# The down products of an MLP block stand two blocks behind its gate and up products instead of one

## The reference, cut to what matters

```
h    = rmsnorm(x_normed, ln1_w)
h    = x_normed + mamba2(h, ...)          # in-projection, conv, scan in chunks of 128, out-projection
h2   = rmsnorm(h, ln2_w)
mlp  = silu(h2 @ gate_w.T) * (h2 @ up_w.T) @ down_w.T      # 512 -> 1792 -> 512
x    = x + layernorm(h + mlp)
# second sublayer: x @ W_up.T plus, for the one of 4 experts that a token picks, a LoRA of rank 8
x    = x + layernorm(ffn(layernorm(x)))
```

## Time and profile before

| | |
|---|---|
| median of 3 executions | 876.89 us (876.71 to 879.94) |
| profiled execution, its own time | 876.88 us |
| its span, first to last instruction | 874.8 us |
| mean granted TensorE clock | 0.965 of full speed |
| PE busy | 793.5 us, 91% |
| DVE busy | 488.4 us, 56% |
| ACT busy | 340.1 us, 39% |
| POOL busy | 201.4 us, 23% |

### The profile page before, as it was taken

One profiled execution on the slowest core, in us unless ns is written; L12 is line 12 of the kernel. 1 busy time (PEld: TensorE's weight loads), 2 busy tenths in 40 slices (PEclk: granted clock), 3 DMA queues, 4 the chain that ended last, 5 costly groups with the idle time before them and its releaser, 6 DMA issues.

```text
span 874.8 us, 15284 instructions
## 1 busy us (share of the span) xinstructions
PE 793.5 (91%) x5712; PEld 557.5 (64%) x5726; DVE 488.4 (56%) x1138; ACT 340.1 (39%) x627; POOL 201.4 (23%) x236
## 2 busy tenths in 40 slices
PE   3857597898999999999999999999999999999945
PEld 3634375566865777567855786567756785677632
DVE  6476565548663576447544665357644765455343
ACT  2443356542552236323651345323632364222211
POOL 3445535531220123101230122002410123000000
PEclk9888789999999999999999999999999999999986
DMA  9920000000000200020001000020002000000010
GB/s 326 386 97 1 1 1 1 25 25 1 1 1 1 73 2 1 1 73 0 0 0 46 26 0 0 0 72 0 0 0 72 0 0 0 24 25 1 2 48 24
DMA packets 15541, 29.70 MB, mean 34 GB/s; under 512 B 1296, under 2 KB 1424, under 8 KB 15504
## 3 DMA queue, kind: packets, MB, share of 16 engines
q1 hardware_dynamic: 15504, 29.21, 9.5%
HBM read 25.01 MB, written 4.19 MB: 33 GB/s over the span
## 4 chain that ended last, share of the span: by engine, by line
PE 63%; issue 13%; DVE 10%; POOL 7%; ACT 4%; DMA 1%; SPq 0%; DVEq 0%; POOLq 0%; ACTq 0%
PE gu L1121 23%; PE wa L1121 19%; PE acc L1121 12%; PE wc L1121 5%; POOL y L445 2%; POOL weights L402 2%; PE wa L1144 2%; POOL ra L429 1%; DVE xbc L879 1%; DMA weights<-in_w_in 1%; DVE sg L965 1%; DVE stats_a L834 1%; DVE hn L856 1%; DVE hn L848 1%; DVE weights L982 1%
## 5 line engine op out<-in xcount | busy, mean ns | idle before, releaser
L1121 PE MATMUL gu<-h2t,weights 128*128 128x256 f16 x2688 | 312.9, 274 | 2.9 <-issue 2.9
L1121 PEld LDWEIGHTS gu<-h2t,weights 128*128 128x128 f16 x2688 | 260.9, 98 | 51.7 <-issue 17.9
L1121 PE MATMUL acc<-weights,act 128*128 128x512 f16 x672 | 165.2, 382 | 13.9 <-DVE act L970 13.9
L965 DVE SCALAR_TENSOR_TENSOR sg<-gu,bound,sg 128x256 f32<-128x256 f32 x112 | 53.5, 478 | 126.5 <-ACT sg L641 126.2
L1121 PE MATMUL wa<-ht,weights 128*128 128x256 f16 x960 | 113.9, 278 | 7.3 <-ACT conv_pad L576 4.3
L1121 PEld LDWEIGHTS wa<-ht,weights 128*128 128x128 f16 x960 | 95.7, 100 | 26.5 <-ACT conv_pad L576 4.5
L1121 PEld LDWEIGHTS acc<-weights,act 128*128 128x128 f16 x672 | 65.0, 98 | 72.2 <-DVE act L970 16.0
L641 ACT ACTIVATE sg<-gu,scale_inv 128x256 f32<-128x256 f32 x112 | 53.1, 474 | 146.5 <-PE gu L1121 146.3
L651 ACT ACTIVATE act<-sg 128x256 f16<-128x256 f32 x112 | 46.6, 416 | 139.8 <-DVE sg L965 138.9
L879 DVE SCALAR_TENSOR_TENSOR xbc<-conv_pad,conv_ws,xbc 128x256 f32<-128x256 f32 x144 | 65.8, 498 | 41.7 <-ACT conv_pad L576 31.5
L970 DVE TENSOR_TENSOR act<-sg,act 128x256 f16<-128x256 f32 x112 | 51.2, 457 | 54.9 <-ACT act L651 54.9
(11 more groups left out here) (182 smaller groups left out, 918.0 us busy)
## 6 DMA issues: line engine op xcount, KB each, us to landing
xa<-in_x SPq DMA_DIRECT2D x8, 512.0 KB, 3.5
weights<-in_x SPq DMA_DIRECT2D x8, 512.0 KB, 4.1
out_x<-h SPq DMA_DIRECT2D x16, 256.0 KB, 2.1
weights<-in_w_gate SPq DMA_DIRECT2D x3, 1024.0 KB, 13.1
weights<-in_w_up SPq DMA_DIRECT2D x3, 1024.0 KB, 14.5
weights<-in_w_down SPq DMA_DIRECT2D x3, 1024.0 KB, 13.9
weights<-in_w_in SPq DMA_DIRECT2D x5, 512.0 KB, 7.1
w_out_t<-in_w_out SPq DMA_DIRECT2D x1, 1024.0 KB, 15.3
```

What stands on the lines that cost most here:

```text
L965: nc.vector.scalar_tensor_tensor(sg[:, f % 2], GU[f % 2][:, SEQ:2 * SEQ], up_to_act, sg[:, f % 2], ALU.mult, ALU.mult).then_inc(sem("prod_ ...
L1121: return nc.tensor.matmul(dst, left, right, start=start, stop=stop)
```

## The change

On PE alone, the order within stage B changes. `b_down(f)` is issued after `b_gu(f + 2)` instead of after `b_gu(f + 1)`. Block 1 no longer has a `b_down` in it, and two of them stand behind block 13. No instruction is added or taken away, and the other engines' queues stay as they are.

```
                     if b is not None:
                         b_gu(b, f)
-                        if f:
-                            b_down(b, f - 1)
+                        if f >= 2:
+                            b_down(b, f - 2)
                     if a is not None and f in A_AT:
                         A_AT[f](a)
                     if c is not None and f in C_AT:
                         C_AT[f](c)
                 if b is not None:
+                    b_down(b, FBLK - 2)
                     b_down(b, FBLK - 1)
```

## The result

The changed kernel takes 884.20 us (median of 5, 883.08 to 885.03), the kernel before 877.76 us in the same comparison (median of 5). The ratio is 1.0072, with a 95% interval of 1.0054 to 1.0090: slower by 6.3 us, between 4.7 and 7.9. The forecast was 884.7 us and +7.8. The profiled execution took 884.76 us, its span is 883.0.

A forecast was written before the change was run, and what follows sets the result against it. PE's matmuls and few waits were taken as the bound, PE being busy 94.21 of 95.30 us in a full step. Terms 7.8 + 0.9 - 0.86 = +7.8 on 876.88 gave 884.7 us, eight-in-ten range 879.5 to 887.5.

The forecast's parts named there:

- The start of steps 2 to 7, +1.30 us each: Before `a_t1`: PE arrives 1.30 us earlier but `hn` does not, so the wait grows from 0.35 to 1.65 us.
- The middle of a step, nothing: Middle of a full step: between A's pieces PE still does one gate and up block and one down product; no change.
- The stalls of step 1: Step 1: PE's 13.2 us of waits for `act` stay as waits for A's inputs or other work; nothing gained.
- The clock term of step 1, +0.9 us: Step 1: PE restarts later, at 111.02, so gate and up 2 runs at low clock; +0.25 to +1.5, taken as +0.9 us.
- The end, -0.9 us: Last step with a B: down 13's wait for `act` goes, covered by downs 11 and 12; -0.86 us.
- The reading of the 2.24 us stall: Before 204.70: the clock stayed at 1.00 after 2.24 us, so the 1.65 us waits were given no clock loss.
- One small sum of the rivals: Step 1, its stalls partly on the path: some 4 or 5 of 13.2 us come back, about 879.5 us; chance 0.07.

The follow-up runs named there:

- The start alone: Kernel before, with no down product in block 1 and two in block 2, the rest in the old order: 886.91 us, ratio 1.0117.
- three blocks: Changed kernel with down products three blocks behind in every step: 886.96 us, ratio 1.0112 to the kernel before.
- the five kernels with moves on DVE: Kernels reordering DVE's queue (centring and scaling before block 0's product, statistics before `b_mlp`, or both), one or two blocks behind: ratios 0.9984, 1.0187, 1.0073, 0.9905, 1.0055.
- The end alone: Kernel before, with only down 12 moved behind `a_t2`, next to down 13: 876.98 us against 876.60, ratio 1.0000.
- Step 1 only: Down products two blocks behind in step 1 alone, one block behind elsewhere as in the kernel before: 877.12 us against 877.13, ratio 1.0001.
- Filling the wait: Changed kernel with 28 more unused matmuls on PE between gate and up 1 and `a_t1` of step 1: 881.54 us, ratio 1.0060 to the kernel before.
- the fastest kernel: Changed kernel with DVE's centring and scaling ahead of block 0's product and statistics ahead of `b_mlp`: 868.25 us, ratio 0.9905 to the kernel before.

## Why the prediction was right, and where it was off

**The start of steps 2 to 7, +1.30 us each: right, and shown.** The trace has 7.9 us in the six steps where the sum had 7.8, and the wait is 1.67 us (1.49 in step 2) where 1.65 was forecast. *The start alone* shows the place, *three blocks* the size of the next wait, the five kernels with moves on DVE the cause: `hn` stands in DVE's queue behind a product that hangs on PE's own gate and up 0, so PE cannot come to it sooner by leaving work out.

**The middle of a step, nothing: right.** *The end alone* leaves a full step at 95.30 us.

**The stalls of step 1: right in kind.** None of the 13.2 us came back; they joined the waits for `hn`, `ra` and the scan, as the growth of these in the waits after shows. The prediction said that an A piece waits there for DVE; the profile names POOL for `ra` and for the scan's `hn`. *Step 1 only* gives a ratio of 1.0001.

**The clock term of step 1, +0.9 us: mis-sized.** The step said "between 114.4 and 116.9" for the end of the low clock, and its bounds were +0.25 to +1.5. Measured in the trace were +1.8, of which 1.56 lie in gate and up 2 (its start to the next start: 4.74 us against 3.18). The clock was 0.50 from 111 to 116 and 0.91 from 116 to 120, so it was low until 116.7, which is 6.1 us after PE's restart at 110.63. Before, it was 5.9 us after the restart at 108.00. The prediction had this 5.9 from the same place and the 3.4 from another stall, and took the middle; the upper value was the right one. The rest was not foreseen: the 5.42 us wait before the scan and the one of 2.06 us drop the clock twice more, and gate and up 9 at 172.82 takes 3.73 us. PE, slowed there, reaches the out-projection at 184.20 with no wait for `y` before it, 13.05 us after the scan's product at 171.15; in *three blocks*, where the clock held, `y` ends the wait 12.74 us after it (168.51 to 181.25). So the second drop costs 0.3 us. *Filling the wait* takes 3.0 us out of the trace.

**The end, -0.9 us: right** (-0.86 in the trace). The experiment that was to show it alone was built on too simple a picture, as told above.

**The reading of the 2.24 us stall was too strong.** The prediction took from one row that a stall of this length leaves the clock alone. *The end alone* has the same stall with the clock falling. For the six full steps of the changed kernel this made no difference, they kept a clock of 1.00 behind 1.67 us; in step 1 the pause of 2.06 us lost it. Of 2.24 us the five profiles show both outcomes, of 2.06 us seven do, and no run here settles at what length the loss begins.

**The total.** The sum of +7.8 stands against +6.3 by the ratio (4.7 to 7.9) and +7.9 between the two profiled executions. The terms of the trace add up to 8.2. Part of the difference is the choice of execution: the profiled one has the longest span of the changed kernel's five, 1.2 us above their median of 881.8, while the 874.8 before is also the median of 21 spans of that kernel. By the medians of the spans the loss is 7.0 us. What is left is smaller than step 1's term, which the runs of *step 1 only* do not show in the time either; the clock behind the 2.24 us stall is a possible reason, not a settled one. That the forecast met the profiled difference to 0.1 us is in part luck: step 1's term was 0.9 us too small there, and the part ahead of it (-0.4), the part behind the last down product (-0.2) and the time outside the span (-0.3) took it back. One small sum of the rivals is off: with 4 or 5 us of step 1 gained back the time would be 879.7 to 880.7, not 879.5.

## What to carry to other kernels

Before work is taken out from between two points of the busiest engine, look at which wait has the least slack behind it, and what starts that wait's chain: if the chain starts at the same engine's work just ahead, leaving out filler buys nothing, and the filler has to be paid for elsewhere. A longer software delay gives slack to one consumer (`act`) and takes cover from another (`hn`); it pays only when the freed slack is then spent, here by letting the other queue put the uncovered producer first. And where stalls are merged rather than removed, count the low clock from the later restart: the matmuls that ran between the stalls no longer help to bring it back, and others pay for it.

## What the runs showed of the hardware

The same pause of PE of 2.24 or 2.25 us at the end of step 1 left the granted clock at 1.00 in two profiles and brought it to 0.79, from 203 to 211 us, in three, which made two gate and up blocks some 1.6 us longer (7.01 to 7.07 against 5.40). A pause of 2.06 us lost the clock in five profiles and kept it in two. With a pause of 2.33 us it fell in all four steps that have one, and with 1.67 us in none from 208 to 780 us.

After a pause of 7.6 us the clock was back at full speed 6.1 us after PE's restart, after one of 4.6 us 5.9 us after it: in these two the longer pause hardly lengthened the low clock behind the restart, it moved it.

POOL's two small operations for the factor took 0.66 and 1.26 us where they ran beside DVE's centring and scaling (393.6 to 395.7 us in the fastest kernel), and 0.19 and 0.69 us just ahead of them. In the kernel before, the pair beside the centring took 0.19 and 0.92 us.
